# Sixteen-head ALiBi attention: the narrow heads' chunks placed between the wide heads' chunks, and a fourth buffer for the stacked queries and keys

## The chip, the cores and the metric

The kernel runs on one core of one Trainium2 chip. The metric is the device time of one execution in microseconds (us), the median of several runs; lower is better.

## What is computed

The whole program is one transformer layer: attention with linear position biases (ALiBi), a residual and layer norm, and then a routed feed-forward part with eight experts. The change touches the attention alone.

```python
B, L, D = 2, 2048, 256; n_heads = 16; head_dim = 16
qkv = (x @ Wqkv + bqkv).reshape(B, L, 3, n_heads, head_dim)
scores = einsum('bqhd,bkhd->bhqk', q, k) / sqrt(head_dim)
scores = scores + slopes[h] * -|pos_q - pos_k|        # slopes[h] = 2 ** (-h / 2)
probs = softmax(scores); out = einsum('bhqk,bkhd->bqhd', probs, v) @ Wout + bout
x = layernorm(x + out); x = layernorm(x + experts(x))
```

## The kernel before

The program has three parts. The **projection** makes queries, keys and values; queries and keys are split into three bfloat16 parts in the tiles `split` (L615, L620, L702), squared for a bound on the scores (L863), and written to memory as `qk_parts`. The **attention** follows, and then the **route and experts** part, which starts with the output projection (PE, L1419) and the rows that VectorE adds from it (L1478, L1480).

In the attention an **item** is one head of one batch; `ITEMS` has 32 of them. A score whose distance times the slope is over 104 is left out, so a head with a steep slope only needs a band around the diagonal. Heads 8 to 15 are wide (all or nearly all of the 2048 x 2048 scores), heads 0 to 7 are narrow (head 0 needs 112 columns on either side of a 128-key block, head 7 needs 1184). The order of the items is pairs: heads 8, 0, 9, 1, and so on to 15, 7, first for batch 0 and then for batch 1.

All scores of an item, transposed (keys in the partitions, queries in the columns), are laid one after another into **chunks** of `WIDTH` = 1536 columns, three PSUM banks. `CHAIN` lists the chunks, `packed` makes it. For each chunk c the engines do the following.

- TensorE (PE) computes the scores, `score(c)`, L987: four matmuls (32 keys each) for every rectangle that `score_cuts` gives. A cut stands at each bank boundary and where a key block's own diagonal begins or ends, so a chunk of a wide head has 3 to 5 rectangles, and one of head 0 has 15 or 16. It waits until chunk c - 2 has been exponentiated, since the two sets of three banks alternate.
- ScalarE (ACT) takes the exponential of the whole chunk into `prob` (L1031), a ring of eight.
- VectorE (DVE) and GpSimd (POOL) multiply the 128x128 blocks on the diagonal by `near_bias` (L1045), even key blocks on VectorE and odd ones on GpSimd.
- PE multiplies by the values, `pv(c - 4)`, L1011, right behind `score(c)`. The sums of an item lie in PSUM bank 6 or 7.
- When an item's last `pv` is done, VectorE copies the sums out (`take`, L1053, bank to `o_sum`), spreads the denominators (L1059), takes four reciprocals (L1064) and scales (L1070); SyncE stores the result. `DIVIDE` places these seven steps, one for each chunk slot: the take at slot `LAST[n] + 6`, the others behind it.

Queries and keys of an item are loaded by SyncE into one of `STACKS` = 3 buffer pairs `q_stack`, `k_stack` (L259 to L293): eleven DMAs for an item. The values are copied by GpSimd into one of two tiles `v_head` (L1098). In program order SyncE alternates: load item n, store item n - 3.

In the words of the code, `FIRST[n]` and `LAST[n]` are the first and last chunk of item n. The chain of before has 489 chunks; the wide head 8 of batch 0 has chunks 0 to 20, head 0 has 20 to 24, head 9 begins in chunk 24. The take of an item frees its bank for the item two places on, and the wait for it stands in `pv`: `pe.wait_ge(o_read, n - 1)`.

## Time and profile before

| | us |
|---|---|
| median of 3 runs | 1063.8 (1063.44 to 1067.05) |
| the profiled execution | 1064.59 |
| its span | 1062.8 |
| PE busy | 1015.1 (96% of the span) |
| ACT busy | 811.9 (76%) |
| exponentials (L1031), 489 of them | 660.6 busy |
| VectorE busy | 453.5 (43%) |
| GpSimd busy | 321.1 (30%) |

The profiled execution is 0.8 us above the median, and 1.8 us of it lie outside the span. The attention fills the stretch from the first exponential at 114.2 us to the last at 785.0 us. A busy PE means only that some matmul is in flight; matmuls of different column groups overlap.

### The profile page before, as it was taken

How to read it: one execution, taken by the hardware profiler on the slowest of the kernel's cores; microseconds unless marked ns; L12 is line 12 of the kernel's file. 1: busy time of each engine (PE TensorE's matmuls, PEld its weight loads, DVE VectorE, ACT ScalarE, POOL GpSimd, SP SyncE). 2: the span in 40 equal slices, each digit the busy share in tenths (PEclk: the TensorE clock that was granted, in tenths of full speed). 3: DMA queues.
4: the chain of work that ended last, by engine and by line, in shares of the span. 5: the costliest groups of instructions: out<-in, count | busy, mean ns of one | idle time of the engine just before them, and what ended most of it. 6: DMA issues, size and time to landing. Idle time of an engine off the chain costs nothing. (4 is left out here: it accounts for less than half of the span.)

```text
span 1062.8 us, 40378 instructions
## 1 busy us (share of the span) xinstructions
PE 1015.1 (96%) x17922; PEld 720.6 (68%) x17922; DVE 453.5 (43%) x1064; ACT 811.9 (76%) x807; POOL 321.1 (30%) x486
## 2 busy tenths in 40 slices
PE   9999899999999999999999999999997399999997
PEld 6555576776676776877666776868686256666665
DVE  5778324564352432325355624323257611111165
ACT  3564799999999999999999999999966164211152
POOL 3333122234121121112232721211330255555433
PEclk9999999999999999999999999999999599999999
DMA  6755312212222111112332221120209246544473
GB/s 195 222 189 173 110 57 72 58 59 83 53 67 61 51 46 46 47 45 68 103 109 64 53 82 54 49 65 25 87 12 301 48 135 174 125 116 113 114 282 133
DMA packets 76562, 104.87 MB, mean 99 GB/s; under 512 B 13774, under 2 KB 62556, under 8 KB 76380
## 3 DMA queue, kind: packets, MB, share of 16 engines
q1 hardware_dynamic: 65852, 87.94, 26.6%
q0 software_dynamic: 6080, 9.06, 4.1%
q10 hardware_dynamic: 4448, 5.19, 1.5%
q8 instruction: 144, 2.36, 0.9%
q14 instruction: 38, 0.31, 0.1%
HBM read 66.49 MB, written 31.48 MB: 92 GB/s over the span
## 5 line engine op out<-in xcount | busy, mean ns | idle before, releaser
L1031 ACT ACTIVATE prob<-ps 128x1536 f32<-128x1536 f32 (+5 forms) x489 | 660.6, 1533 | 13.4 <-PE ps L987 12.1
L987 PE MATMUL ps<-q_stack,k_stack 111*32 111x512 bf16 (+25 forms) x9308 | 467.3, 302 | 7.0 <-issue 5.1
L1011 PE MATMUL ps<-prob,v_head 128*32 128x128 f32 (+6 forms) x7288 | 467.6, 338 | 2.5 <-issue 2.5
L987 PEld LDWEIGHTS ps<-q_stack,k_stack 111*32 111x32 bf16 (+2 forms) x9308 | 257.2, 96 | 132.2 <-ACT prob L1031 70.5
L1011 PEld LDWEIGHTS ps<-prob,v_head 128*32 128x32 f32 x7288 | 291.0, 110 | 53.4 <-issue 4.9
L1045 POOL TENSOR_TENSOR prob<-prob,near_bias 128x128 f32<-128x128 f32 x288 | 141.7, 496 | 500.6 <-ACT prob L1031 497.5
L1045 DVE TENSOR_TENSOR prob<-prob,near_bias 128x128 f32<-128x128 f32 x288 | 97.9, 348 | 400.4 <-ACT prob L1031 399.2
L1064 DVE RECIPROCAL o_rec<-o_den 128x128 f32<-128x128 f32 x128 | 113.8, 924 | 0.7
L1744 PE MATMUL ps<-xeT,w 128*128 128x512 f32 x224 | 99.2, 601 | 0.8 <-ACT xeT L1775 0.7
L1821 ACT ACTIVATE hT<-ps 128x512 f32<-128x512 f32 x28 | 16.7, 596 | 106.5 <-PE ps L1744 106.5
L1758 PE MATMUL ps<-w,hT 128*128 128x256 f32 x448 | 97.9, 379 | 0.0
L1758 PEld LDWEIGHTS ps<-w,hT 128*128 128x128 f32 x448 | 84.8, 190 | 11.5 <-issue 0.5
L1744 PEld LDWEIGHTS ps<-xeT,w 128*128 128x128 f32 x224 | 43.1, 193 | 52.9 <-issue 50.6
L502 PE MATMUL ps<-xT,w_qkv 128*128 128x512 f32 x128 | 60.1, 599 | 1.0 <-DVE w_qkv L740 1.0
L615 ACT ACTIVATE split<-ps,bias_qk_columns 128x512 bf16<-128x512 f32 x32 | 22.0, 687 | 44.3 <-PE ps L502 42.0
L1979 DVE TENSOR_SCALAR hT<-ps 128x512 f32<-128x512 f32 x28 | 19.4, 692 | 79.7 <-PE ps L1744 79.7
L863 POOL TENSOR_TENSOR square<-split 128x512 bf16<-128x512 bf16 x32 | 33.6, 1050 | 64.0 <-ACT split L615 63.9
L2032 POOL DMA_INDIRECT token_sums<-ye,slot_token x20 | 31.6, 1578 | 60.4 <-DVE ye L1995 42.3
L2012 POOL DMA_INDIRECT xe<-z_rows,slot_token x28 | 28.4, 1013 | 52.6 <-DVE slot_token L1582 44.4
L502 PEld LDWEIGHTS ps<-xT,w_qkv 128*128 128x128 f32 x128 | 23.6, 190 | 23.1 <-issue 19.4
L1995 DVE TENSOR_SCALAR ye<-ps,slot_weights 128x256 f32<-128x256 f32 x20 | 9.7, 484 | 65.5 <-PE ps L1758 65.5
L511 PEld LDWEIGHTS ps<-w_qkv,xT 128*128 128x128 f32 x128 | 24.1, 190 | 14.6 <-issue 10.5
(175 smaller groups left out, 610.7 us busy)
## 6 DMA issues: line engine op xcount, KB each, us to landing
qk_parts<-split SPq DMA_DIRECT2D x32, 384.0 KB, 3.0
w<-L_ffn_experts_inter_dram SPq DMA_DIRECT2D x7, 1024.0 KB, 6.4
w<-n_L_ffn_experts_out_dram SPq DMA_DIRECT2D x7, 1024.0 KB, 9.5
q_stack<-qk_parts SPq DMA_DIRECT2D x31, 192.0 KB
k_stack<-qk_parts SPq DMA_DIRECT2D x31, 192.0 KB
z_rows<-v SPq DMA_DIRECT2D x8, 516.0 KB, 8.8
heads<-o_out SPq DMA_DIRECT2D x128, 32.0 KB, 2.4
v<-in_L_attn_x_dram SPq DMA_DIRECT2D x8, 512.0 KB, 6.8
```

The lines of the kernel that those rows point to most:

```text
L502: mm = pe.matmul(ps[:, 2 + m, :], w[:, k, m * P:(m + 1) * P], xT[n % 2][:, k, :], start=(k == 0), stop=(k == 1))
L511: mm = pe.matmul(ps[:, 6 + s % 2, 0:DX], xT[n % 2][:, k, s * P:(s + 1) * P], w[:, k, 2 * D:3 * D + EXTRA], start=(k == 0), stop=(k == 1))
L863: pool.tensor_tensor(square[m][:, :], split[m][:, 0, :], split[m][:, 0, :], ALU.mult)\
L987: mm = pe.matmul(ps[k:k + 32, SLOT_BANKS * (c % 2) + bank, col:col + z - a], k_st[n % STACKS][0:rows, kb * P + k:kb * P + k + 32], q_st[n ...
L1011: mm = pe.matmul(ps[32 * g:32 * g + 32, 6 + n % 2, column:column + width * times], vh[n % 2][:, kb, :], moving, start=(n, g) not in begun, ...
L1031: act.activation(prob[:, c % RING, 0:at + z - a], ps[:, bank:bank + SLOT_BANKS, :].rearrange("p c n -> p (c n)")[:, 0:at + z - a], ACT.Exp ...
L1045: eng.tensor_tensor(here, here, near[:, h, :], ALU.mult).then_inc(done, 1)
L1064: dve.reciprocal(o_rec[:, mine], o_den[:, mine]).then_inc(o_step, 1)
L1744: mm = pe.matmul(ps[:, 2 + j % 2, :], w1[par][:, k, j * P:(j + 1) * P], xeT[par][:, k, :], start=(k == 0), stop=(k == 1))
L1758: mm = pe.matmul(ps[:, 4 + s, 0:D], hT[:, j, s * P:(s + 1) * P], w2[par][:, j, :], start=(j == 0), stop=(j == FT - 1))
L2012: pool.indirect_dma_start(out=xe[e % 2][:, s, :], out_offset=None, in_=z_rows, in_offset=bass.IndirectOffsetOnAxis(ap=t["slot_token"][:, e ...
L2032: pool.indirect_dma_start(out=acc_rows, out_offset=bass.IndirectOffsetOnAxis(ap=t["slot_token"][:, e, s:s + 1], axis=0), in_=ye[e % 2][:, ...
```

## The change

The chain is made anew. `woven` lays out one pair of items: the wide head's chunks from column 0 on, so that their pieces stand on bank boundaries more often; the narrow head's are laid out by `evenly`, which makes them equally wide and so mostly shorter than 1536 columns. Behind the wide head's fourth chunk at the earliest, the narrow head's chunks are put between the wide ones, spread over its length. Pairs do not overlap in the chain, and no chunk is shared between pairs. The chain has 494 chunks.

An item now ends in another order than it begins, so takes, divides and stores go by `ENDING` and `RANK` (the narrow item of a pair ends first, three chunks before the wide one), and an item's PSUM bank and value tile are `place_of(n)`: a wide item takes the place that the narrow item before it leaves. Both items of a pair are live at once, so there are four stacks. The fourth lies in the `split` tiles of the projection; its first load waits for `parts_out`. The stores stay three items behind the loads (`STORE_LAG`). The shift rows of batch 1 (`part_shift`, `widen_shift` on VectorE) move from the start of the attention to slots 6 to 8. The four bias additions of batch 1 on GpSimd (`BIAS_AT`) stand in the last 13 chunks. In the general path, which does not run here, a semaphore is reused.

```diff
-STACKS = 3
+STACKS = 4
+STORE_LAG = 3
+NARROW_FROM = 4
+SHIFT_SLOT = 6
-def packed(items):
...
+def evenly(n, h, at):
+    columns = at + sum(z - a for _, a, z in spans(h, 0))
+    count = -(-columns // WIDTH)
+    widths = range(-(-columns // count // 16) * 16, WIDTH, 16)
+    return fill(n, h, at, 0, next((w for w in widths if w >= at and len(fill(n, h, at, 0, w)) == count), WIDTH))
+def woven(wide, narrow):
+    first = fill(*wide, 0, 0)
+    at = sum(z - a for *_, a, z, _ in first[-1])
+    second = evenly(*narrow, at)
+    wide_chunks, narrow_chunks = first[:-1], [first[-1] + second[0]] + second[1:]
+    chunks, done = [], 0
+    for r, chunk in enumerate(wide_chunks):
+        chunks.append(chunk)
+        due = max(0, r + 2 - NARROW_FROM) * len(narrow_chunks) // (len(wide_chunks) - NARROW_FROM - 2)
+        chunks += narrow_chunks[done:due]
+        done = max(done, due)
+    return chunks
-CHAIN = packed(ITEMS)
+CHAIN = [chunk for n in range(0, len(ITEMS), 2) for chunk in woven((n, ITEMS[n][1]), (n + 1, ITEMS[n + 1][1]))]
+ENDING = sorted(range(len(ITEMS)), key=lambda n: LAST[n])
+RANK = [ENDING.index(n) for n in range(len(ITEMS))]
+def place_of(n):
+    return (n // 2 + n % 2) % 2
-BIAS_AT = [FIRST[-8] + 3 * c for c in range(QG)] + [FIRST[-1] + 3 * c for c in range(QG)]
+BIAS_AT = [FIRST[-8] + 3 * c for c in range(QG)] + [CHUNK_COUNT - 13 + 3 * c for c in range(QG)]
-            n = LAST.index(slot - VALUE_LAG - 2)
+            n = RANK[LAST.index(slot - VALUE_LAG - 2)]
-                    if n >= 2:
-                        pe.wait_ge(o_read, n - 1)
+                    if place_user_before(n) is not None:
+                        pe.wait_ge(o_read, RANK[place_user_before(n)] + 1)
-            dve.wait_ge(pv_done, LAST[n] + 1)
+            dve.wait_ge(pv_done, LAST[ENDING[n]] + 1)
-        part_shift(dve, t, 1, 4)
-        for part in range(3):
-            widen_shift(dve, t, 1, part)
         for slot, steps in enumerate(DIVIDE):
+            if slot == SHIFT_SLOT:
+                part_shift(dve, t, 1, 4)
+            if 0 <= slot - SHIFT_SLOT < 3:
+                widen_shift(dve, t, 1, slot - SHIFT_SLOT)
+            split = v_life.enter_context(nc.sbuf_tensor("split", [P, 4, 3, CH], BF16))
+            t["split"] = [split[:, m, :, :] for m in range(4)]
+            spare = split[0:ROWS, :, :, :].rearrange("p m c n -> p (m c n)")
+            t["q_stack"].append(spare[:, 0:L])
+            t["k_stack"].append(spare[:, L:2 * L])
```

**PE, head 0 of batch 0.** Before, the scores of chunks 21 and 22 stand one behind the other, with only a value product of head 8 between them (`q_stack1` is head 0's stack, `v_head0` head 8's values; each row is a score rectangle's four matmuls, or value products):

```order
L987 MATMUL ps<-q_stack1,k_stack1 32x128 x4
L987 MATMUL ps<-q_stack1,k_stack1 32x112 x8
L1011 MATMUL ps<-prob,v_head0 32x384 x3
L1011 MATMUL ps<-prob,v_head0 32x128
L1011 MATMUL ps<-prob,v_head0 32x256
L987 MATMUL ps<-q_stack1,k_stack1 32x128 x4
L987 MATMUL ps<-q_stack1,k_stack1 32x112 x8
```

In the change, on PE at the same head, the end of chunk 10 (head 0), the wide chunk 11 and the wide chunk 12:

```order
L1015 MATMUL ps<-q_stack1,k_stack1 32x64 x4
L1039 MATMUL ps<-prob,v_head0 32x256 x2
L1039 MATMUL ps<-prob,v_head0 32x384 x2
L1015 MATMUL ps<-q_stack0,k_stack0 32x128 x4
L1015 MATMUL ps<-q_stack0,k_stack0 32x384 x4
L1015 MATMUL ps<-q_stack0,k_stack0 32x512 x8
L1039 MATMUL ps<-prob,v_head0 32x128 x3
L1039 MATMUL ps<-prob,v_head0 32x256 x4
L1039 MATMUL ps<-prob,v_head0 32x128
L1015 MATMUL ps<-q_stack0,k_stack0 32x512 x4
```

What moved: three full score chunks of head 0 in a row (15, 15 and 16 rectangles) have become four chunks of 14 or 15 rectangles (1328 or 1360 columns), at places 10, 14, 18 and 21, with two or three chunks of head 8 between them. Over the whole attention the score matmuls fall from 9308 to 8832 and the value products go from 3644 to 3660 (each is two rows of the profile, since float32 passes count twice).

**VectorE, the end of the attention.** Before, the last item is divided alone, behind its last diagonal block (`o_sum1` holds the last item's sums, `extra0` is the first row of the route part):

```order
L1045 TENSOR_TENSOR prob<-prob,near_bias 128x128 x3
L1053 COPY o_sum1<-ps 128x512
L1059 STREAM_SHUFFLE o_den<-o_sum1 128x512
L1064 RECIPROCAL o_rec<-o_den 128x128 x4
L1070 TENSOR_TENSOR o_out1<-o_sum1,o_rec 128x512
L1467 MEMSET eps 128x1
L1478 TENSOR_TENSOR extra0<-ps,v 128x36
```

In the change, VectorE at the same place (`o_sum0` is head 7 of batch 1, `o_sum1` head 15):

```order
L1073 TENSOR_TENSOR prob<-prob,near_bias 128x128 x9
L1081 COPY o_sum0<-ps 128x512
L1087 STREAM_SHUFFLE o_den<-o_sum0 128x512
L1092 RECIPROCAL o_rec<-o_den 128x128
L1081 COPY o_sum1<-ps 128x512
L1092 RECIPROCAL o_rec<-o_den 128x128 x3
L1098 TENSOR_TENSOR o_out0<-o_sum0,o_rec 128x512
L1087 STREAM_SHUFFLE o_den<-o_sum1 128x512
L1092 RECIPROCAL o_rec<-o_den 128x128 x4
L1098 TENSOR_TENSOR o_out1<-o_sum1,o_rec 128x512
L1496 MEMSET eps 128x1
L1507 TENSOR_TENSOR extra0<-ps,v 128x36
```

What moved: two items end in chunks 490 and 493, so both are divided behind the last diagonal block, where one was before (it ended in chunk 488, the other in chunk 469).

**VectorE, a change of pairs.** In the change, VectorE after pair 8, 0 of batch 0 (the take into `o_sum0` is head 1's; the next into `o_sum1` is head 9's, three slots on):

```order
L1073 TENSOR_TENSOR prob<-prob,near_bias 128x128 x8
L1081 COPY o_sum0<-ps 128x512
L1087 STREAM_SHUFFLE o_den<-o_sum0 128x512
L1092 RECIPROCAL o_rec<-o_den 128x128
L1073 TENSOR_TENSOR prob<-prob,near_bias 128x128
L1081 COPY o_sum1<-ps 128x512
```

What stands behind this: the bank of the narrow item must be read before the next wide item's first `pv`. The distance `FIRST[n]` minus `LAST` of the bank's user before is 4 chunks at all fifteen changes of pairs now. Before it was 4 at the first change of each batch and 5 or more at the others.

## Rows read from the trace of the kernel before

**Rows 1.** The page: span, busy time of each engine, and the tenths in 40 slices.
```profile
span 1062.8 us, 40378 instructions
PE 1015.1 (96%) x17922; PEld 720.6 (68%) x17922; DVE 453.5 (43%) x1064; ACT 811.9 (76%) x807; POOL 321.1 (30%) x486
...
ACT  3564799999999999999999999999966164211152
```
**Rows 2.** The exponentials (L1031): duration ns min/median/max, first and last start; idle before.
```profile
L1031 ACT ACTIVATE prob<-ps x489: 317/1525/1720, 114.2 to 785.0; 128x1536 f32<-128x1536 f32 x154, 128x1440 f32<-128x1440 f32 x3, 128x1504 f32<-128x1504 f32 x2, 128x1456 f32<-128x1456 f32 x1
...
  PE ps L987: 12.1, 16
```
**Rows 3.** ACT timeline (start, us busy, idle before): groups of exponentials, startup and head 0's.
```profile
114.17 5.48 ACT L1031 ACTIVATE prob<-ps 128x1536 f32<-128x1536 f32 x4 [2.89 <-PE ps L987]
119.88 1.45 ACT L1031 ACTIVATE prob<-ps 128x1536 f32<-128x1536 f32 x1 [0.23 <-PE ps L987]
122.16 23.09 ACT L1031 ACTIVATE prob<-ps 128x1536 f32<-128x1536 f32 x17 [0.82 <-PE ps L987]
...
126.36 5.49 ACT L1031 ACTIVATE prob<-ps 128x1536 f32<-128x1536 f32 x4
...
149.83 11.00 ACT L1031 ACTIVATE prob<-ps 128x1536 f32<-128x1536 f32 x8 [1.07 <-PE ps L987]
```
**Rows 4.** ACT timeline, single chunks: starts of chunks 33, 42, 204, 244 and 448.
```profile
162.03 13.57 ACT L1031 ACTIVATE prob<-ps 128x1536 f32<-128x1536 f32 x10
...
174.00 2.95 ACT L1031 ACTIVATE prob<-ps 128x1536 f32<-128x1536 f32 x2
...
395.51 1.49 ACT L1031 ACTIVATE prob<-ps 128x1536 f32<-128x1536 f32 x1
...
449.29 1.45 ACT L1031 ACTIVATE prob<-ps 128x1536 f32<-128x1536 f32 x1
...
731.17 1.49 ACT L1031 ACTIVATE prob<-ps 128x1536 f32<-128x1536 f32 x1
```
**Rows 5.** Waits of PE from 130 to 787 us: total us, times, longest.
```profile
PE ps L987 <- issue: 3.6, 8, 1.0
PE ps L1011 <- issue: 2.5, 4, 1.1
```
**Rows 6.** PE's matmuls in stretches from one such stop to a later one.
```profile
145.10:149.00 3.90, 2.85 (x127) 1.00 0.40 120
149.00:182.70 33.70, 33.20 (x882) 1.00 0.23 63
182.70:223.60 40.90, 40.76 (x1134) 1.00 0.26 71
...
516.40:520.50 4.10, 3.68 (x126) 1.00 0.36 107
520.50:524.40 3.90, 3.70 (x127) 1.00 0.23 80
```
**Rows 7.** The page: the queue that brings instructions (packets, MB, share).
```profile
q8 instruction: 144, 2.36, 0.9%
```
**Rows 8.** PE timeline, wide head 8: two score groups and two value groups.
```profile
128.02 0.88 PE L987 MATMUL ps<-q_stack,k_stack 111*32 111x512 bf16 x16
128.68 0.88 PE L1011 MATMUL ps<-prob,v_head 128*32 128x128 f32 x16
129.33 0.89 PE L987 MATMUL ps<-q_stack,k_stack 123*32 123x128 bf16 x20
```
**Rows 9.** VectorE timeline at the take of head 8 of batch 0.
```profile
151.31 0.76 DVE L1045 TENSOR_TENSOR prob<-prob,near_bias 128x128 f32<-128x128 f32 x2 [1.77 <-ACT prob L1031]
152.00 0.68 DVE L1053 COPY o_sum<-ps 128x512 f32<-128x512 f32 x1
```
**Rows 10.** VectorE and PE timelines at the end of the attention.
```profile
787.40 0.69 DVE L1053 COPY o_sum<-ps 128x512 f32<-128x512 f32 x1 [1.97 <-PE ps L1011]
...
788.89 3.39 DVE L1064 RECIPROCAL o_rec<-o_den 128x128 f32<-128x128 f32 x4
792.32 0.69 DVE L1070 TENSOR_TENSOR o_out<-o_sum,o_rec 128x512 f32<-128x512 f32 x1
...
793.04 1.21 DVE L1480 TENSOR_TENSOR v<-ps,v 128x1024 f32<-128x1024 f32 x1
...
787.29 3.85 PE L1419 MATMUL ps<-w_out,heads 128*128 128x265 f32 x16
792.49 0.69 PE L1419 MATMUL ps<-w_out,heads 128*128 128x265 f32 x2 [1.35 <-DVEq L1088]
```
**Rows 11.** All engines from 118 to 130 us; the figure 0.86 is PE's granted clock.
```profile
118.00:130.00 12.00, 11.64 (x222) 7.61 (x224) 0.88 (x3) 10.87 (x9) 1.37 (x3) 0.86 0.32 106
```
**Rows 12.** SyncE timeline: the load of item 1's stack, first and last DMA.
```profile
113.12 2.04 SPq L259 DMA_DIRECT2D q_stack<-qk_parts  x3
...
119.29 0.28 SPq L293 DMA_DIRECT2D q_stack<-shift_rows  x1
```

More of the change, by code:

```diff
@@ L111, in filled @@
     return max((at + z - a for _, _, a, z, at in chunk), default=0)
-def packed(items):
-    chunks = [[]]
-    for n, (b, h) in enumerate(items):
-        at = filled(chunks[-1])
-        mine = next(new for new in (fill(n, h, at, more) for more in range(0, P, 16))
-                    if n + 1 == len(items) or filled(new[-1]) % P == 0)
-        chunks = chunks[:-1] + [chunks[-1] + mine[0]] + mine[1:]
-        if filled(chunks[-1]) == WIDTH:
-            chunks.append([])
-    return [chunk for chunk in chunks if chunk]
+def evenly(n, h, at):
[15 more added lines that the diff above has]
+    return chunks
 def own_column(piece):
@@ L181, with place_user_before @@
 FIRST, LAST = [uses[0] for uses in USES], [uses[-1] for uses in USES]
+ENDING = sorted(range(len(ITEMS)), key=lambda n: LAST[n])
+RANK = [ENDING.index(n) for n in range(len(ITEMS))]
+def place_of(n):
+    return (n // 2 + n % 2) % 2
+def place_user_before(n):
+    earlier = [m for m in range(len(ITEMS)) if place_of(m) == place_of(n) and LAST[m] < FIRST[n]]
+    return max(earlier, key=lambda m: LAST[m]) if earlier else None
 def own_blocks(c, odd):
     return [(ITEMS[piece[0]][1], own_column(piece)) for piece in CHAIN[c] if own_column(piece) is not None and piece[1] % 2 == odd]
-BIAS_AT = [FIRST[-8] + 3 * c for c in range(QG)] + [FIRST[-1] + 3 * c for c in range(QG)]
+BIAS_AT = [FIRST[-8] + 3 * c for c in range(QG)] + [CHUNK_COUNT - 13 + 3 * c for c in range(QG)]
 def value_bursts():
@@ L955, in banded_sync @@
                   .then_inc(t["shift_out"], 16)
-            if n >= STACKS:
-                store_turned_heads(n - STACKS)
-            if 0 <= n - (H + STACKS) < QG:
+            if n >= STORE_LAG:
+                store_turned_heads(n - STORE_LAG)
+            if 0 <= n - (H + STORE_LAG) < QG:
                 sp.wait_ge(vh_done, H)
-                load_rows(sp, n - (H + STACKS))
-            if n == H + STACKS:
+                load_rows(sp, n - (H + STORE_LAG))
+            if n == H + STORE_LAG:
                 for buf in range(2):
@@ L964, in banded_sync @@
                 sp.sem_inc(t["heads_ready"], 1)
-        for n in range(len(ITEMS) - STACKS, len(ITEMS)):
+        for n in range(len(ITEMS) - STORE_LAG, len(ITEMS)):
             if n == len(ITEMS) - 2:
@@ L1010, in pv @@
                     moving = slab[:, at:at + width]
-                mm = pe.matmul(ps[32 * g:32 * g + 32, 6 + n % 2, column:column + width * times],
-                               vh[n % 2][:, kb, :], moving, start=(n, g) not in begun, stop=False,
+                mm = pe.matmul(ps[32 * g:32 * g + 32, 6 + place_of(n), column:column + width * times],
+                               vh[place_of(n)][:, kb, :], moving, start=(n, g) not in begun, stop=False,
                                skip_group_check=True)
@@ L1095, in banded_gpsimd @@
                 b, h = ITEMS[n]
-                if n >= 2:
-                    pool.wait_ge(pv_done, LAST[n - 2] + 1)
-                pool.tensor_copy(vh[n % 2][:, :, 0:HD], t["v"][:, b * KB:(b + 1) * KB, h * HD:(h + 1) * HD])\
+                if place_user_before(n) is not None:
+                    pool.wait_ge(pv_done, LAST[place_user_before(n)] + 1)
+                pool.tensor_copy(vh[place_of(n)][:, :, 0:HD], t["v"][:, b * KB:(b + 1) * KB, h * HD:(h + 1) * HD])\
                     .then_inc(vh_done, 1)
@@ L1190, in general_scalar @@
         for h in range(ONE_SIDED, H):
-            act.activation(near[:, h, :], dist[:, :], ACT.Exp, scale=nslope[:, h:h + 1]).then_inc(near_both, 1)
-        act.sem_inc(expd, 2 * CHUNKS)
+            act.activation(near[:, h, :], dist[:, :], ACT.Exp, scale=nslope[:, h:h + 1]).then_inc(expd, 1)
+        act.sem_inc(expd, 2 * CHUNKS - (H - ONE_SIDED))
         with act.Fori(0, H) as h:
@@ L2136, in build @@
                 t[name] = v_life.enter_context(nc.sbuf_tensor(name, shape, F32))
-            t["q_stack"] = [v_life.enter_context(nc.sbuf_tensor(f"q_stack{k}", [ROWS, L], BF16)) for k in range(STACKS)]
-            t["k_stack"] = [v_life.enter_context(nc.sbuf_tensor(f"k_stack{k}", [ROWS, L], BF16)) for k in range(STACKS)]
+            t["q_stack"] = [v_life.enter_context(nc.sbuf_tensor(f"q_stack{k}", [ROWS, L], BF16)) for k in range(STACKS - 1)]
+            t["k_stack"] = [v_life.enter_context(nc.sbuf_tensor(f"k_stack{k}", [ROWS, L], BF16)) for k in range(STACKS - 1)]
             t["stack_in"] = [v_life.enter_context(nc.semaphore(f"stack_in{k}")) for k in range(STACKS)]
@@ L2142, in build @@
                 t[name] = v_life.enter_context(nc.sbuf_tensor(name, shape, dt))
-            t["split"] = [v_life.enter_context(nc.sbuf_tensor(f"split{m}", [P, 3, CH], BF16)) for m in range(4)]
+            split = v_life.enter_context(nc.sbuf_tensor("split", [P, 4, 3, CH], BF16))
[3 more added lines that the diff above has]
+            t["k_stack"].append(spare[:, L:2 * L])
             t["parts_out"] = [v_life.enter_context(nc.semaphore(f"parts_out{m}")) for m in range(4)]
```

12 lines of the change are left out of this document (6 added, 6 removed).

## The prediction

> **What bounds the kernel now.** I read the page first: PE is busy for 96% of the span and ACT for 76%, and over the whole attention ACT's slices show 9 tenths or more [rows 1]. A busy PE only says that some matmul is in flight, so the row of the exponentials comes next: 489 of them, the first at 114.2, the last starting at 785.0 us [rows 2]. That is 670.8 us for 488 steps. In an undisturbed stretch, chunks 33 and 42 start at 162.03 and 174.00 [rows 4]: nine steps in 11.97 us, 1.33 us each, and ACT waits for nothing. At that pace 488 steps take 649.0 us. 22 chunks ahead of the last are short, by 1,440 columns together. The exponential of 128 columns takes 0.317 us and that of 1536 columns 1.45 us [rows 2, 3], 0.80 ns a column, so 1.2 us come off: 647.8 us. **ACT loses 23.0 us to PE in the attention**; these are the only microseconds that a new order of the chunks can win there.
>
> Where they lie: chunk 0 starts at 114.17, chunk 4 at 119.88, chunk 5 at 122.16 [rows 3]. With the step after it, 1.5 us are lost here, before any narrow head; from 118 to 130 us PE's granted clock was 0.86 on average [rows 11], a time at the 1.2 GHz level behind a quiet PE. The order of chunks 0 to 5 is the same in the change, so I keep these 1.5 us. In pairs 14, 6 (ends) and 15, 7, chunk 204 starts at 395.51, chunk 244 at 449.29, chunk 448 at 731.17 and chunk 488 at 785.0 [rows 2, 4]: 40 steps take 53.78 and 53.8 us against 53.0 for their columns, a thin loss of 0.02 us a step. Over 488 steps that is 9.8 us. What is left, 23.0 - 1.5 - 9.8 = **11.7 us**, lies at the steep heads. Head 0 shows it: chunk 5 starts at 122.16 and chunk 24 at 149.83, 19 steps in 27.67 us where 25.3 would do, and 1.07 us of plain idle stand before chunk 24 [rows 3].
>
> What stops PE there: its waits from 130 us on are all put down to issue, 12 of them, 6.1 us [rows 5]. No engine released them. Counting the matmuls from one such stop to the next gives the cause: 127, 882 and 1134, and 126 and 127 later on, that is 1, 7, 9, 1 and 1 times 126 [rows 6]. A matmul has a weight load beside it, so 126 are 252 instructions, and with the semaphore instructions about 256. The instruction queue moved 144 packets in 2.36 MB, 16.4 KB each [rows 7], 64 bytes for each of 256. So PE stops at a boundary of instruction blocks, where the next block has not landed, and a block that is run through faster than it can be fetched takes 3.9 to 4.1 us [rows 6]. Before, a chunk of head 0 has 60 score matmuls and 26 passes of values, 86 in all, and four in a row are 2.7 blocks: over 10 us where ACT needs 5.3. A wide chunk has about 28, or 4.5 chunks and 6 us to a block.
>
> The Trainium skill (Runtime: NRT & Kernel Launch, Instruction fetch mechanics) says the sequencer fetches 16 KiB blocks of 256 instructions by itself, one ahead, and that crossing a boundary is mostly hidden. The block size agrees with the packets here; that it is hidden does not, at these heads. If it were hidden, nothing of the 6.1 us would come back and the gain below would shrink to what PE's longer small matmuls cost.
>
> **The parts, and their costs.**
>
> *More and shorter chunks.* 493 steps at 1.33 are 655.7 us. The chunks lack 11,200 columns now, at 0.80 to 0.83 ns 9.0 to 9.3 us: 646.5 us against 647.8. **-1.3 us**, if PE keeps the pace. It has little to spare: in a wide chunk it starts scores at 128.02, values at 128.68, the next scores at 129.33 [rows 8], a round of 1.31 us against ACT's 1.33. Narrow chunks cost it more, in the change as before, but fewer cuts in the wide ones (476 score matmuls less) give about as much back. The thin loss stays, 0.02 x 493 = 9.9 us.
>
> *Narrow between wide (the 11.7 us).* One chunk of head 0 (about 80 matmuls) and three wide ones are 165 matmuls, 1.3 blocks: at 3.9 us a block 5.1 us, and ACT needs 3 x 1.33 + 1.18 = 5.2. On average the fetch just holds. But the block with the narrow chunk in it holds 80 and 46 of 1.6 wide chunks, 1.4 + 1.6 x 1.33 = 3.5 us, against 3.9. So up to 0.4 us is late for each chunk with 12 or more rectangles, of which there are 16: 0 to 6.4 us remain. PE may be late by a little before ACT feels it: the exponential of chunk 8 runs from 126.36 for 1.45 us, to 127.81, and PE starts the scores that wait for it at 128.02, 0.2 late; yet the four exponentials from 126.36 fill 5.49 us, which is ACT's full pace [rows 3, 8]. I take **1.5 us**.
>
> *The wait for the bank.* At all fifteen changes of pairs `pv(FIRST)` waits for a take that stands in slot FIRST + 2 on VectorE, behind the diagonal block of that same chunk. PE gets to this `pv` 0.05 + 0.66 us after that exponential's end. VectorE needs about 0.38 for the block and 0.68 for the copy [rows 9], with the semaphores 1.1 us. So PE is 0.35 to 0.4 late, and so is everything behind it on its queue: the scores of the next chunk, for which ACT waits. Of this 0.2 to 0.3 is covered by the slack above, and PE wins back 0.02 a chunk. Between nothing and 15 x 0.4 = 6 us; I take 0.11 each, **+1.7 us**, near the low end, since the row with lateness and a full pace is at hand.
>
> *The end of the attention.* Before, the last exponential (128 columns) ends at 785.3 and VectorE's last scale at about 793.0 [rows 2, 10], 7.7 us later: four value products, then 5.6 us for one item's division. The route part begins behind it on the same engine, and PE waits for it too: the matmul at 792.49 has 1.35 us idle ahead [rows 10]. In the change VectorE has two divisions, 11.2 us, and the first cannot begin before `pv(490)`, two rounds of 0.66 into the exponential of the chunk before last or so, 0.6 us ahead of the last exponential's end. It ends 10.6 us behind that end: **+2.9 us**. And the last chunk is full, 1.45 instead of 0.32: **+1.1 us**. Nothing covers either.
>
> *Loads, shift rows, biases: nothing.* Item 1's stack is wanted at chunk 10, near 127.5 us. Its DMAs go out from 113.12 to 119.6 [rows 12] and need some us to land. Later loads have 16 chunks, 21 us, for 6.5 us of issue. The same bytes move. The shift rows go to slots 6 to 8, where VectorE idles; they did not hold the first block up either. If the stack of item 1 came late, ACT would lose that lateness once.
>
> *Sum.* First exponential 114.2 + 646.5 + 9.9 + 1.5 + 1.5 + 1.7 = 775.3 for the start of the last, 776.8 for its end, 787.4 for VectorE's end, against 793.0: **-5.6 us**, and with roundings I say -5.9. All behind shifts with it. The profiled execution took 1064.59, 0.8 over the median of 1063.8; the difference carries over: **1057.9 us**.
>
> **The rivals.**
>
> *The fetch holds and the bank's wait is hidden* (0.20). Then 1.5 and 1.7 fall away: 1054.7; if the thin loss shrinks too, by the better cuts, some us lower, 1051. For it: averages of 5.1 against 5.2 us, and the slack. Against: the single block does not hold.
>
> *The stops stay, smaller and more of them* (0.14). Each of some 16 steep chunks pays 0.4, and those of heads 4 and 5 a little: 5 to 6 us instead of 1.5, 1062. For it: stacks are loaded while narrow chunks run, and the blocks took 4.1 us at 516 with DMA share 0.36 but 3.9 at 520 with 0.23 [rows 6].
>
> *The clock drops at the end* (0.08). PE now idles some 5 us before the output projection instead of 1.35 [rows 10], and after the quiet before 118 us it fell to 1.2 GHz for a while [rows 11]. The second 3.85 us group of the projection would then take up to twice as long, and VectorE waits for it: up to 3.9 us, 1061.5.
>
> *Slower: the take comes late* (0.07). If at a change of pairs VectorE is still in a reciprocal (3.39 us for four [rows 10], 0.85 each) when the block and the take are due, PE is 1.2 late and ACT loses 0.9 a time. At over 0.5 us a change, 15 times, the 5.9 are gone: at 0.9, 13.5 - 1.7 = 11.8 more, 1069.7. Against: the steps of the pair before end long before, and the narrow item's own begin behind its take.
>
> The change does what it says, so I keep no chance for that.
>
> **How the numbers follow.** The forecast holds 0.51. Its own range is 1054.5 to 1061. Together with the second and third cases it covers 8 in 10 from 1051 to 1063; to take in part of the slow one I say 1050.5 to 1064. A measurement of this kernel tells about 0.5%, 5.3 us, from no change: the bound is 1058.5. The forecast lies on the fast side of it in six of ten cases (0.31), the first rival always (0.20): faster 0.51. Slower by over 0.5%, over 1069.1, only the last: 0.05. Same: 0.44.
>
> **What would show it.** PE's issue waits between 130 and 787 us fall from 6.1 to under 3 us, and stand single at narrow chunks. Chunk 25 starts near 149 us, and the exponentials start last at 774 to 777. PE or its weight loads wait for VectorE's take, some 0.3 us, at up to fifteen places. VectorE has about 10.6 us from the end of the last exponential to its first row addition. The prediction is wrong if the last exponential starts outside 768 to 781, or if the way from there to the row additions is not 11 to 13 us.

## The result: 3.7% slower

The changed kernel takes 1104.14 us (median of 4 runs, 1101.86 to 1105.11) against 1063.74 us (4 runs, 1063.44 to 1067.05) of the kernel before on the same chip: a ratio of 1.037, 95% interval 1.034 to 1.040. The profiled execution took 1103.84 us, its span is 39.2 us longer than that of [rows 1].

The page of the changed kernel: span, busy times, ACT's tenths and PE's granted clock in 40 slices, then the rows of the exponentials (L1059) and of one form of the scores (L1015), with the idle time before them behind the bar.

```profile
span 1102.0 us, 39505 instructions
...
PE 1022.3 (93%) x17478; PEld 751.9 (68%) x17478; DVE 454.5 (41%) x1064; ACT 812.0 (74%) x812; POOL 323.4 (29%) x486
...
ACT  3654899879999999997796999999975255111152
...
PEclk9999999989999999998998999999998679999999
...
L1059 ACT ACTIVATE prob<-ps 128x1536 f32<-128x1536 f32 (+4 forms) x494 | 660.7, 1463 | 46.1 <-PE ps L1015 45.8
...
L1015 PE MATMUL ps<-q_stack,k_stack 111*32 111x512 bf16 (+16 forms) x6800 | 400.4, 322 | 35.3 <-DMA split<-shift_rows 16.3
```

ACT computes as long as before (660.7 us), and idles 45.8 us for PE in place of 12.1 [rows 2]. Its slices had 9 tenths or more all through the attention [rows 1]; now there are two dips, one early in each batch. The steep heads come first in a batch, so the dips lie where a pair is short.

The view of waits, PE from 130 to 818 us (total us, times, longest), in the places of [rows 5]:

```profile
PE ps L1015 <- DMA split<-shift_rows: 16.3, 4, 6.7
PE ps L1015 <- DMA q_stack<-shift_rows: 12.9, 6, 5.2
PE ps L1039 <- DVE o_sum L1081: 1.9, 3, 1.6
PE ps L1015 <- issue: 0.2, 1, 0.2
```

The 12 waits put down to issue, 6.1 us, have become one of 0.2: that part of the forecast came true. In their place stand ten waits, 29.2 us, for a load of a query and key stack; `shift_rows` is the last of its eleven DMAs. e1 below shows that this is what made the kernel slower.

One of these waits in three views. SyncE's timeline: the store of head 1 of batch 0, the load of item 6 (head 11), first and last DMA, the store of head 9, and the load of item 7 (head 3), first and last DMA.

```profile
204.98 2.62 SPq L964 DMA_DIRECT2D heads<-o_out  x4
207.65 1.96 SPq L287 DMA_DIRECT2D q_stack<-qk_parts  x3
...
213.47 0.28 SPq L321 DMA_DIRECT2D q_stack<-shift_rows  x1
213.79 2.79 SPq L964 DMA_DIRECT2D heads<-o_out  x4
216.63 2.77 SPq L287 DMA_DIRECT2D split<-qk_parts  x3
...
223.64 0.27 SPq L321 DMA_DIRECT2D split<-shift_rows  x1
```

The DMA view of 216 to 224 us, some of the load's DMAs (KB each):

```profile
split<-qk_parts SPq DMA_DIRECT2D x2, 192.0 KB
split<-qk_parts SPq DMA_DIRECT2D x2, 128.0 KB
...
split<-shift_rows SPq DMA_DIRECT2D x1, 12.0 KB
```

PE's and ACT's timelines there:

```profile
230.57 0.85 PE L1039 MATMUL ps<-prob,v_head 128*32 128x384 f32 x8 [0.18 <-DVE o_sum L1081]
236.41 0.62 PE L1015 MATMUL ps<-q_stack,k_stack 123*32 123x384 bf16 x8 [4.98 <-DMA split<-shift_rows]
...
237.84 1.36 ACT L1059 ACTIVATE prob<-ps 128x1424 f32<-128x1424 f32 x1 [5.66 <-PE ps L1015]
```

PE is ready for head 3's first scores at 231 us and gets them at 236.4; ACT idles 5.66 us behind it. The load takes 7.3 us to issue, and another 12.5 from its last DMA, which moves 12 KB, until PE goes on: 19.8 us in all. It went out so late because of what stands ahead of it on SyncE's queue. SyncE waits for VectorE's division of head 1, which ends at 204.96 us; then it issues that store, the load of item 6 and the store of head 9, 11.7 us together. The division of head 9 ended at 211.67, while SyncE was still busy with the load of item 6, so this second store waits for nothing. SyncE's waits, 112 to 830 us:

```profile
SPq L964 <- DVE o_out L1098: 409.6, 19, 35.3
SPq L287 <- PE ps L1015: 8.2, 14, 2.3
```

Nearly all of SyncE's waiting time is now for a division, not for a free stack. In program order it has load n, store n - 3, load n + 1. The narrow item's division of a pair finishes 10 to 12 chunks into the next pair, the wide one's 16. The first holds back the next wide load. The narrow load begins 9 to 10 us after that one, behind its issue and one more store. But a narrow item is now wanted 4 to 6 chunks behind its wide one (10 in the first pair of a batch), where before the wide item's 20 or more chunks lay between. The load of a late narrow item begins 11 or 12 chunks, 15 to 16 us, ahead of its first exponential, and takes 18 to 21 us. In five short pairs PE waits 3.5 to 6.7 us for it.

Long pairs lose little. From the starts of the exponentials, against 1.33 us a step less the missing columns as the prediction counts them, the five pairs with heads 2 and 3 of batch 0 and heads 1, 2 and 3 of batch 1 (26 to 29 chunks each) lose 5.6, 7.8, 9.0, 9.0 and 9.8 us; the pairs with heads 5, 6 and 7 (33 to 40 chunks) lose 0.6 to 1.4 each.

The clock adds to it. The view of windows (us, busy time with instructions, PE's granted clock, DMA share, GB/s), three stretches of the changed kernel:

```profile
220.00:240.00 20.00, 14.84 (x294) 9.13 (x290) 4.93 (x13) 13.54 (x11) 4.70 (x11) 0.83 0.17 58
480.00:500.00 20.00, 19.52 (x530) 15.46 (x526) 7.06 (x16) 19.54 (x15) 5.09 (x11) 1.00 0.31 95
500.00:520.00 20.00, 15.66 (x395) 10.64 (x390) 8.92 (x17) 13.56 (x11) 3.73 (x8) 0.83 0.08 20
```

With each of the four waits of 4.3 to 6.7 us, the trace's record of PE's clock has the 1.2 GHz level in place of 2.4 for 6.8 us, from 1.8 to 4.4 us into the wait on; behind the wait of 3.5 us it has 3.4 us of it. The mean over 20 us is then 0.83 or 0.91. The waits of 1.6 us or less have none. The length of the wait alone doesn't decide it: in other profiles 3.4 us at this level began beside or behind waits of 2.8 us (e9), 2.4 us (e5) and 1.9 us (e10), while the first profile of the change has none behind its wait of 2.5 us at 126 us. So a stall can cost more than its length. In the pair of the wait shown, PE's wait is 5.0 us and ACT loses 7.8, where it loses 0.8 in e2 below. Over the attention the ten waits are 29.2 us and the exponentials take 41 us longer than in e1 and e2; that all of the other 12 us are the clock's isn't shown.

The end of the attention, VectorE, beside [rows 10]:

```profile
819.76 0.63 DVE L1081 COPY o_sum<-ps 128x512 f32<-128x512 f32 x1
820.30 2.56 DVE L1092 RECIPROCAL o_rec<-o_den 128x128 f32<-128x128 f32 x3
822.89 0.69 DVE L1098 TENSOR_TENSOR o_out<-o_sum,o_rec 128x512 f32<-128x512 f32 x1
...
828.25 0.87 DVE L1098 TENSOR_TENSOR o_out<-o_sum,o_rec 128x512 f32<-128x512 f32 x1
829.05 0.18 DVE L1507 TENSOR_TENSOR extra<-ps,v 128x36 f32<-128x36 f32 x1
...
835.08 0.20 DVE L1507 TENSOR_TENSOR extra<-ps,v 128x36 f32<-128x36 f32 x1 [4.71 <-PE ps L1448]
```

and PE there:

```profile
819.21 3.85 PE L1448 MATMUL ps<-w_out,heads 128*128 128x265 f32 x16
828.43 11.91 PE L1448 MATMUL ps<-w_out,heads 128*128 128x265 f32 x40 [5.37 <-DVEq L1117]
```

The whole ledger, from starts and ends in the two traces: the first exponential starts 0.5 us earlier (113.7 against 114.2); from there to the last 702.4 us against 670.8, +31.7; from the last exponential's start to the output projection 3.1 against 2.3, +0.8; the projection from its first matmul to its last 37.2 against 30.5, +6.7 (4.0 of it longer idling, 5.37 against 1.35; the other 2.7 go with 6.8 us at the 1.2 GHz level, which begin 4 us into that idling); everything behind +0.5. Together +39.2.

### The profile page after: what moved, and what is told of

It is laid out like the page before. It is cut to its first block and busy times, and to the rows that moved or that the text cites. A ratio compares the mean times of both kernels' runs of the same rounds, so it can differ in the third digit from the quotient of the medians.

```text
span 1102.0 us, 39505 instructions
## 1 busy us (share of the span) xinstructions
PE 1022.3 (93%) x17478; PEld 751.9 (68%) x17478; DVE 454.5 (41%) x1064; ACT 812.0 (74%) x812; POOL 323.4 (29%) x486
## 5 line engine op out<-in xcount | busy, mean ns | idle before, releaser
L1059 ACT ACTIVATE prob<-ps 128x1536 f32<-128x1536 f32 (+4 forms) x494 | 660.7, 1463 | 46.1 <-PE ps L1015 45.8
L1039 PE MATMUL ps<-prob,v_head 128*32 128x128 f32 (+7 forms) x7320 | 486.0, 340 | 2.4 <-DVE o_sum L1081 1.9
L1015 PE MATMUL ps<-q_stack,k_stack 111*32 111x512 bf16 (+16 forms) x6800 | 400.4, 322 | 35.3 <-DMA split<-shift_rows 16.3
L1039 PEld LDWEIGHTS ps<-prob,v_head 128*32 128x32 f32 x7320 | 300.9, 110 | 45.2 <-issue 14.1
L1015 PEld LDWEIGHTS ps<-q_stack,k_stack 111*32 111x32 bf16 (+2 forms) x6800 | 223.2, 97 | 125.7 <-ACT prob L1059 43.3
L1092 DVE RECIPROCAL o_rec<-o_den 128x128 f32<-128x128 f32 x128 | 114.9, 927 | 0.7
L1787 PEld LDWEIGHTS ps<-w,hT 128*128 128x128 f32 x448 | 84.7, 190 | 11.7 <-issue 0.5
L1015 PE MATMUL ps<-split 123*32 123x512 bf16 (+35 forms) x2032 | 83.9, 273 | 0.0
L1015 PEld LDWEIGHTS ps<-split 123*32 123x32 bf16 (+2 forms) x2032 | 57.0, 97 | 16.6 <-ACT prob L1059 7.9
```

The lines of the kernel that those rows point to most:

```text
L1015: mm = pe.matmul(ps[k:k + 32, SLOT_BANKS * (c % 2) + bank, col:col + z - a], k_st[n % STACKS][0:rows, kb * P + k:kb * P + k + 32], q_st[n ...
L1039: mm = pe.matmul(ps[32 * g:32 * g + 32, 6 + place_of(n), column:column + width * times], vh[place_of(n)][:, kb, :], moving, start=(n, g) n ...
L1059: act.activation(prob[:, c % RING, 0:at + z - a], ps[:, bank:bank + SLOT_BANKS, :].rearrange("p c n -> p (c n)")[:, 0:at + z - a], ACT.Exp ...
L1092: dve.reciprocal(o_rec[:, mine], o_den[:, mine]).then_inc(o_step, 1)
L1787: mm = pe.matmul(ps[:, 4 + s, 0:D], hT[:, j, s * P:(s + 1) * P], w2[par][:, j, :], start=(j == 0), stop=(j == FT - 1))
```

## The experiments

e1 to e4 ran on a chip on which the kernel before takes 1070.1 us, e5 to e7 on one with 1070.4, e8 and e9 on a third, e10 and e11 on a fourth. So kernels are compared by their ratios to the kernel before on their own chip, and by stretches inside the attention.

**e1_lag4: the stores four items behind the loads.** SyncE's order becomes load n, store n - 4, load n + 1, so the division that is waited for is an earlier one.

```diff
-STORE_LAG = 3
+STORE_LAG = 4
```

> One number of the change: STORE_LAG 4 instead of 3, so SyncE no longer waits for the division of the wide item before it issues the load of the next pair's narrow item (item 5's load could go out at slot 35 to 40 instead of 46). Theory 1 (late stacks: the load of a narrow item stands on SyncE behind a store that waits for a division, and takes 18 us and more from its first DMA to its landing): the waits of PE for stacks, 29 us after 130 us, go to under 2 us, only item 1's 2.6 us stay; the last exponential starts near 776 instead of 816; about 1064 us. Rival A (the fourth stack in the projection's buffers, or its DMAs, is slow by itself): waits at items with stack 3 stay, 16 us; 1085 or more. Rival B (the woven order itself costs PE, by small matmuls and lost clock): under 10 us gained.

Measured: 1067.93 us, ratio 0.998 (0.996 to 0.9995). The expected 1064 was on the first chip's scale; this one takes 6 us more for the kernel before. PE's waits from 130 to 775 us:

```profile
PE ps L1039 <- DVE o_sum L1081: 2.1, 4, 1.6
PE ps L1039 <- issue: 0.5, 1, 0.5
PE ps L1015 <- issue: 0.2, 1, 0.2
```

No wait for a stack is left there, and the exponentials go from 114.6 to 776.4 us. One number takes away the whole loss (1.037 to 0.998) and leaves the chain, the fourth stack in `split`, the banks and the bytes as they are. So the order on SyncE's queue is the cause, and the theory that the fourth stack's place or more traffic was to blame falls. The order of the chunks, unchanged here, loses nothing by itself; it only set the earlier deadline.

**e2_pairs: both items of a pair loaded together**, as soon as the wide item two pairs back has been scored, then both stores.

```diff
-        for n, (b, h) in enumerate(ITEMS):
...
+        for pair in range(STACKS, len(ITEMS), 2):
+            for n in (pair, pair + 1):
+                load_item(n)
+            for n in (pair, pair + 1):
+                store_turned_heads(n - STACKS)
...
```

> The change with another order on SyncE alone: both items of a pair are loaded one behind the other, as soon as the wide item two pairs back is scored, and the two stores follow them. Narrow items' loads go out some 9 slots after their pair's stacks are free, so they have over 25 slots. Theory 1: no waits for stacks but item 1's 2.6 us, no clock drops in the attention, last exponential near 776, about 1063 us; the remaining difference to the kernel before is then the end of the attention, some 8 us lost (two divisions and the clock), against 8 to 9 us won in the chunks. Rival B: over 1080 us.

Measured: 1066.77 us, ratio 0.997 (0.996 to 0.999). SyncE's waits from 130 to 700 us are now mostly for a free stack, which is what a load must wait for:

```profile
SPq L287 <- PE ps L1019: 163.8, 19, 27.1
SPq L964 <- DVE o_out L1102: 85.4, 27, 5.9
```

The exponentials go from 113.8 to 774.2 us, the prediction's 114.2 to 775.3 to about a microsecond. The forecast's total for the chain of chunks came out, given stacks that are there in time; its terms did less well, as shown below.

**e3_from8: the change's order on SyncE, but the narrow items begin later** (`NARROW_FROM` 8 in place of 4). A dose test: each narrow item begins 2 to 4 chunks, 3 to 5 us, later.

```diff
-NARROW_FROM = 4
+NARROW_FROM = 8
```

> One number of the change: NARROW_FROM 8 instead of 4, so a narrow head's first chunk stands 3 to 5 chunks (4 to 5.3 us) later behind its wide head's start; SyncE's order is as in the change. Theory 1: each wait for a stack shrinks by what the chunk moved: items 1, 5, 9, 19 and 25 to nothing, item 7 from 6.0 to about 0.7, item 21 from 5.9 to 1.9, item 23 from 7.5 to 2.2 us; with the clock drops that go with them about 1070 us. Rival (the DMA queues are overrun, so that later use finds later stacks): the waits keep their size, 1095 or more.

Measured: 1071.66 us, ratio 1.003 (1.001 to 1.004); PE's waits from 130 to 775 us:

```profile
PE ps L1015 <- DMA q_stack<-shift_rows: 4.2, 4, 1.4
...
PE ps L1015 <- DMA split<-shift_rows: 1.5, 1, 1.5
```

5.7 us of waits are left of 29.2, none of over 1.5 us, and the first exponential to the last takes 666.3 us. Waits of 3.5 to 6.7 us became 0 to 1.5.

**e4_cut: the kernel before, with head 15 of batch 0 scored in cuts of 128 columns.** It adds 660 matmuls to a pair that had no such stops before, at the same columns. It tests the step that the prediction put in the place of the skill's rule.

```diff
+    if n0 == 14:
+        ends |= {c for c in range(0, L, P) if a < c < z}
```

> The kernel before with the scores of one wide item (head 15 of batch 0, 21 chunks) cut into rectangles of 128 columns: 48 score matmuls for a chunk instead of 12 to 20, 660 more in all, the same columns and results. It measures the instruction stops by themselves. If PE's stops are the fetch of instruction blocks, 21 chunks of some 62 matmuls are 10.3 blocks of 126, and they take 3.4 to 3.9 us each: 35 to 40 us for the item instead of 28, with issue stops 126 matmuls apart; 7 to 12 us slower than before. If small matmuls alone cost (0.0125 us a rectangle, as narrow chunks show), it is 1 to 2 us slower and has no issue stops there.

Measured: 1077.16 us (four runs, 1070.6 to 1078.1), ratio 1.005 (1.001 to 1.009). The exponentials of the pair with heads 15 and 7 took 63.6 us where the kernel before takes 53.8. PE's waits, 130 to 800 us:

```profile
PE ps L990 <- issue: 9.6, 13, 1.4
PE ps L1014 <- issue: 4.0, 8, 1.1
```

13.6 us against the 6.1 of [rows 5]. Nine of the stops, 6.6 us, lie in the changed pair, 126 to 128 matmuls apart (254 once), as expected for blocks of 256 instructions. More matmuls at the same columns bring such stops where there were none. That fits blocks of instructions used up faster than they arrive; fewer narrow chunks in a row (e1, e2) take the stops away. PE's own extra work on small matmuls is part of the 9.8 us and wasn't measured apart.

**e5_tail: as e2, with the last narrow item ending ten chunks ahead of the end** in place of three, so that one division is left behind the last exponential.

```diff
+    before_end = 9 if wide[0] == len(ITEMS) - 2 else 2
...
-        due = max(0, r + 2 - NARROW_FROM) * len(narrow_chunks) // (len(wide_chunks) - NARROW_FROM - 2)
+        due = max(0, r + 2 - NARROW_FROM) * len(narrow_chunks) // (len(wide_chunks) - NARROW_FROM - before_end)
```

> Kernel e2_pairs with the chunks of the last narrow item ending 10 chunks ahead of the end in place of 3. Theory, that the rest of what the change lost lies behind the last exp (two divisions there, and TensorE idle for 5.4 us ahead of the second output projection, after which its granted clock fell): one division stays behind the end, the row addition starts 8.0 to 9.0 us after the last exp starts in place of 13.0, TensorE waits about 1.4 us there, and there is no record of the lower clock near 783. With the clock's share (2 to 3 us) the time falls by 4 to 8 us, to 1059 to 1063 us on this chip. Rival, that the clock's drop has to do with the change of work at the end of attention and not with TensorE's idle time: the drop stays and the time falls by 4 to 5 us only. Rival, that the narrow's denser chunks cost what the end gains: the last pair loses over 3 us against 0.7, and the time stays at 1066 to 1067 us.

Measured: 1062.76 us, ratio 0.992 (0.990 to 0.994). VectorE's first row addition and the last exponential, PE's output projection:

```profile
787.04 0.19 DVE L1512 TENSOR_TENSOR extra<-ps,v 128x36 f32<-128x36 f32 x1
790.53 0.20 DVE L1512 TENSOR_TENSOR extra<-ps,v 128x36 f32<-128x36 f32 x1 [2.17 <-PE ps L1453]
...
786.60 5.61 PE L1453 MATMUL ps<-w_out,heads 128*128 128x265 f32 x24 [1.99 <-DVEq L1122]
```

From the last exponential's start (777.85) to the row addition are 9.2 us against 13.0 in e2; PE idles 1.99 us and not 5.37; the projection takes 31.1 us where e2's took 36.3, and no stretch at 1.2 GHz begins behind it. It gains 0.5% on e2, at the low end of the forecast. The last pair loses 0.8 us against 0.7, so the rival of the denser chunks falls. In this profile head 0's stack came late by 2.4 us, with 3.4 us at the 1.2 GHz level behind it; the first pair loses 4.7 us and not 2.6, most of the 3.6 us by which its last exponential stands behind that of e2. e7 deals with it.

Does PE's idling bring the lower clock there? The windows from 770 to 790 us of this run, and of e7, which has the same end:

```profile
770.00:790.00 20.00, 18.01 (x232) 11.92 (x228) 12.93 (x22) 12.44 (x16) 9.00 (x17) 1.00 0.06 13
```

```profile
770.00:790.00 20.00, 18.02 (x99) 13.78 (x92) 15.19 (x51) 8.46 (x28) 5.09 (x15) 0.91 0.41 127
```

In e7, 3.4 us at 1.2 GHz begin at 778.2, behind the same idling of 1.98 us. Over all profiles: with 5.4 us of idling the lower clock came in six of six, with 2.0 in one of three (e7, not e5 or e11), with 1.35, the kernel before, in none of four. More idling goes with it more often. The rival, the change of work at the end of the attention, isn't excluded.

**e6_take: as e2, with VectorE's take ahead of the diagonal block of its slot.**

```diff
+            for n, step in steps:
+                if step == TAKE:
+                    take(n)
             if slot < CHUNK_COUNT:
                 near_blocks(dve, slot, 0, diag_even)
...
```

> Kernel e2_pairs with VectorE's take of a finished sum put ahead of the near biases of the same slot. Theory, that the first value matmuls of each wide item wait for the take, 0.13 to 0.14 us at each of 15 pairs and 1.6 us in the pair with the bias additions: TensorE's waits for the take vanish (2.1 us in 4 now), the step of exp at 5 chunks after a wide item's first falls from 1.47 to 1.33 to 1.35 us, and the time falls by 2 to 3.5 us. Rival, that these waits are hidden by the ring of eight slots: the waits vanish and the time stays within 0.5 us.

Measured: 1064.13 us, ratio 0.994 (0.993 to 0.996). PE's waits for the take (2.1 us in e2) are gone, and most pairs lose 0.1 to 0.3 us less, the pair in which GpSimd adds the biases 1.6 less. The exponential's step behind each change of pairs is 1.30 to 1.34 us, where e2 has 1.38 to 1.55, and 2.84 in that pair. The exponentials take 656.5 us from first to last against 660.4. So the wait for the bank cost 3.9 us and wasn't hidden.

**e7_all: e5 and e6 together, head 0 of batch 0 begun five chunks later, and the first four bias additions ten chunks later**, off the place where GpSimd copies the next narrow item's values.

```diff
+    start = 9 if wide[0] == 0 else NARROW_FROM
...
+        due = max(0, r + 2 - start) * len(narrow_chunks) // (len(wide_chunks) - start - before_end)
...
-BIAS_AT = [FIRST[-8] + 3 * c for c in range(QG)] + [CHUNK_COUNT - 13 + 3 * c for c in range(QG)]
+BIAS_AT = [FIRST[-8] + 10 + 3 * c for c in range(QG)] + [CHUNK_COUNT - 13 + 3 * c for c in range(QG)]
```

> Kernel e2_pairs with the edits of e5_tail and e6_take, the first narrow item begun 5 chunks later (its stack lands 1.3 us late now), and the first four bias additions 10 chunks later (off the place where the next narrow item's values are copied by the same engine). If the causes add up: 4 to 8 us for the end, 2 to 3 for the take (the 1.6 us of the bias additions among them), 1 to 1.5 for the first item, together 7 to 12 us below e2_pairs, 1055 to 1060 us on this chip, and 10 to 15 us below the kernel before. Rival, that the first pair pays for it in denser chunks at its end: the first pair's loss stays at 2.6 us.

Measured: 1056.49 us, ratio 0.988 (0.986 to 0.990), against 1070.38. The exponentials by source (ns min, median, max; first and last start; idle before):

```profile
L1065 ACT ACTIVATE prob<-ps x494: 1270/1500/1660, 114.6 to 769.1; 128x1536 f32<-128x1536 f32 x128, 128x1504 f32<-128x1504 f32 x9, 128x1408 f32<-128x1408 f32 x8, 128x1424 f32<-128x1424 f32 x6
...
  PE ps L1021: 3.1, 2
```

654.6 us from first to last, 16 less than before, and 3.1 us of idling. The first pair lost 0.7 us in this profile, so here it doesn't pay for the later start; e11 below has the same kernel again. The parts add up: from e2 on 0.9% (10 us) for all edits, where e5 brought 0.5% and e6 0.3% alone.

**e8_before and e9_after: the two kernels themselves, on one more chip.**

> The kernel before itself, unchanged, for a profile on this chip: its runs take 1070 us here and 1064 on the chip of the first comparison. If the 6 us lie behind the end of attention, its span from the first row addition to the end is 274 to 277 us (269.8 on the first chip) and its exp chain is 671 us as there; then the spans behind the end of e1 to e7 (274.3 to 277.4 us) are this chip's and not the edits'. If they lie in attention, the exp chain is 676 to 678 us and the tail 270 us.

> The changed kernel itself, unchanged, for a profile on this chip. Theory of the late stacks: the same seven narrow items' stacks are late (pairs 2, 3, 9, 10 and 11 lose 5.6 to 9.8 us each), TensorE waits 25 to 35 us for stacks, its clock falls behind the waits of over 5 us, and the time is 1108 to 1114 us. Rival, that the waits of the first run were an accident of that chip's transfers: other pairs lose, or fewer than half of the us.

Measured: 1066.49 and 1104.34 us, one run each. e8 has the exponentials from 114.9 to 786.8 and 270.0 us from the first row addition to the end. Its chip runs the kernel before in 1063.3, so it decides nothing about the slower chips. e9 shows the same as the first trace of the change; PE's waits from 130 to 818 us:

```profile
PE ps L1015 <- DMA split<-shift_rows: 15.4, 3, 6.7
PE ps L1015 <- DMA q_stack<-shift_rows: 13.5, 6, 5.0
```

The same five pairs lose 5.0, 7.7, 9.1, 9.1 and 10.0 us. The late stacks are no accident of one run. Its time, 1104, is 4 us under what I expected, for I had added the slower chip's microseconds.

**e10_before and e11_all: what sets the length of the tail.** The span behind the first row addition was 274 to 277 us in e1 to e7.

> The kernel before, unchanged, beside e11_all on one chip. What is open: the span from the first row addition to the end was 274 to 277 us in e1 to e7, whose chips take 1070 us for the kernel before, and 269.8 and 269.9 us in the two profiles of the kernel before, on chips that take 1063 to 1066. If the chip sets it, both kernels of this pair have the same tail within 2 us, long or short as the chip is. If the edits set it, this one has 270 us and e11_all 274 or more.

> Kernel e7_all, unchanged, beside e10_before on one chip. If the chip sets the tail: within 2 us of e10_before's, and the ratio again 0.986 to 0.990. If the edits set it: 274 us or more against 270, and on a chip that takes 1064 us for the kernel before the ratio is 0.988 to 0.992.

Measured: e10 1066.85 us (one run), e11 1052.61 us, ratio 0.988 (0.985 to 0.990) to 1065.92. The tails are 271.0 and 270.4 us, where e7, the same kernel as e11, had 275.5. The seven profiles e1 to e7, on two chips, have 274 to 277 us, the other six, on the other chips, 270 to 273, whatever the kernel. So the chip sets it. Windows of e7, then of e11, the same 20 us:

```profile
860.00:880.00 20.00, 19.92 (x78) 15.83 (x79) 2.06 (x5) 11.75 (x23) 4.60 (x3) 0.91 0.49 154
```

```profile
860.00:880.00 20.00, 19.67 (x82) 15.14 (x83) 2.63 (x5) 12.55 (x24) 4.18 (x3) 1.00 0.53 182
```

e7 has a second stretch at 1.2 GHz there, at the first expert's matmuls, and e11 none. All of e1 to e7 have it, for 3.4 or 6.8 us, and none of the other six. It goes with a longer wait of PE at the same place, 3.5 us in e7 and 1.5 in e11 (2.9 to 4.0 in e1 to e7, 1.5 in the others), so the chips differ in something ahead of the clock. What that is isn't shown.

e11's exponentials take 658.4 us from first to last against e7's 654.6. Its first pair lost 3.3 us where e7's lost 0.7, with no wait for a stack: 1.9 against 0.4 in the first seven chunks, under 6.8 us at 1.2 GHz in place of 3.4, and 1.4 against 0.2 in the last nine, with one issue stop of 0.5 us. So two profiles don't agree on whether the denser chunks at the end of the first pair cost anything. The version of e7 and e11 beats both kernels, the kernel before by 1.2% and the changed one by 4.7% (0.988 / 1.037 = 0.953).

## Why the prediction was wrong

The step that failed is **"Loads, shift rows, biases: nothing"**, in its sentence "Later loads have 16 chunks, 21 us, for 6.5 us of issue." It compared the wrong things. The issue is one part of three. The second is the landing, by the records of the semaphore that each load counts up: 9 to 14 us from the last DMA's issue, so that a load needs 16 to 25 us, and a late narrow one 18 to 21. The trace of before had it: item 1's load landed at 129.0 us, 9.5 after its last DMA, where the prediction has "some us to land". The third is the start: the load goes out behind a store that waits for a division of the pair before, and behind another load, so that it has 11 or 12 chunks and not 16. The prediction looked at SyncE's loads but not at what stands between them on the queue. It cost some 41 us in late stacks and the slow clock behind them (in e1 and e2 the exponentials take 661.8 and 660.4 us from first to last in place of 702.4), against the 9 to 10 us that the new chain gains. It priced a late stack in one sentence, "ACT would lose that lateness once", for item 1 alone. PE waited for a stack ten times from 130 us on. None of the prediction's rivals had this; the slowest of them stood at 1069.7.

The Trainium skill (SBUF — State Buffer, The DMA setup-cost knee) puts a transfer at some 2 us fixed and its bytes at 436 GB/s. An estimate by it, with the load's 984 KB taken as one transfer: it would land 4.3 us after it began, and could not have been late. The small stores here agree with the fixed part, the DMA view of 112 to 830 us gives

```profile
heads<-o_out SPq DMA_DIRECT2D x126, 32.0 KB, 2.6
```

but eleven DMAs behind each other on one queue, and behind the load of item 6, took 19.8 us, about 50 GB/s. The measurement decides: this load of many pieces is far from that estimate. What sets its pace isn't shown.

Point by point, the others:

- *The instruction stops.* Right: 6.1 us of issue waits became 0.2 in the change, 0.7 in e1, none in e2; e11 has 1.4. e4 brought them back where there were none. The Trainium skill's rule that crossing a block is mostly hidden (Runtime: NRT & Kernel Launch, Instruction fetch mechanics) does not hold for PE here at small matmuls. The prediction's "over 10 us" for four chunks of head 0 was too much, though: chunks 20 and 24 start at 142.32 and 149.83 in the trace of before, 7.5 us apart.
- *More and shorter chunks, and the sum of the chain.* Once the stacks are there, the last exponential starts at 774.2 (e2) and 776.4 (e1), forecast 775.3. Such close agreement is partly luck. Counted as the prediction counts, e2 loses 13.8 us in the chain where it had 14.6, but the bank's wait is 3.9 in place of 1.7, a late first stack takes 0.7 in place of nothing, and the thin loss and the steep heads together 7.5 in place of 9.9 + 1.5.
- *The wait for the bank.* The mechanism was right, the size too small: forecast 1.7 us, worth 3.9 us in e6. At ordinary changes of pairs the exponential's step in e2 is 1.38 to 1.55 us in place of 1.33, 0.12 more on average, where 0.11 was forecast. Mis-sized was the pair with the biases, where the take was 1.6 us late behind other work; the rival "the take comes late" had this for all pairs.
- *The end of the attention.* Forecast +2.9 and +1.1, measured +5.0 from the last exponential's start to the row addition (13.0 against 8.0 us): 1.2 for the longer exponential and 3.8 for the second division.
- *The clock drops at the end.* Given 0.08 and up to 3.9 us, it came in both profiles of the change, in e1, e2, e3 and e6, each time with 5.4 us of idling: the projection took 35.9 to 37.4 us against 30.5, of which 4.0 are the idling and 1.4 to 2.9 go with the lower clock. The idling follows from a step that I had taken as certain, so this term belonged into the sum.
- *The start.* The 1.5 us were kept for a clock dip that is not always there: the first profile of the change, e4, e5, e8 and e10 have none before 130 us, e1 to e3, e6, e7, e9 and e11 have 3.4 or 6.8 us of it from 116 to 119 on.
- *The last line of the sum.* The terms give -5.6; the step to -5.9 "with roundings" has no row behind it.

With the failed step mended and nothing else, e2 is the forecast's kernel: ratio 0.997, 1061 us on the scale of the first chip. Of the 3 us to 1057.9, 1.8 go with the lower clock in e2's projection.

## What to carry to other kernels

A load that is wanted earlier must be followed back through three things: when it may go out, what stands ahead of it on its queue and what that waits for, and how long it takes from the first issue until the last byte is there, read from a wait in the trace and not from the issue. An interleaving that puts two consumers closer together moves the deadline of the second's input by the whole length of the first. A stall of a few us on PE can cost its own length and then a stretch at the slow clock. And a total that comes out right doesn't vouch for its terms.

## What the runs showed of the hardware

- A load of eleven DMAs, 984 KB on one queue, is complete 9 to 14 us after its last DMA (12 KB) was issued (in the change 11 to 14 for the narrow items' loads, which follow another load by 3 to 4 us, and 9 to 11 for most others), where the median 32 KB store needs 2.6 us.
- PE's granted clock was at the 1.2 GHz level for 3.4 or 6.8 us with every wait of 3.5 us or more in the attention, and with some of 1.9 to 2.8 us, though PE is busy at over 9 tenths otherwise.
- PE stops for 0.2 to 1.9 us at multiples of about 126 matmuls where small matmuls follow each other, and a pair of heads that had no such stop got nine of them when its matmuls were cut smaller (e4).
- The same kernel has a tail of 275.5 us on one chip and 270.4 on another, with a longer wait of PE (3.5 against 1.5 us) and a second stretch at 1.2 GHz on the first.
